# A gated cross-attention kernel on one core: turns and gate products put behind the projections, and an output bias added by GpSimd

## What is computed

```python
x = x + tanh(g_xattn[0]) * L0_xattn(layernorm(x), ctx)   # one head, 77 keys
x = x + tanh(g_ffn[0])   * L0_ffn(layernorm(x))          # 256 -> 1024 -> 256, quantised
x = x + tanh(g_xattn[1]) * L1_xattn(layernorm(x), ctx)   # 16 heads, out = concat @ Wo + bo
x = x + tanh(g_ffn[1])   * L1_ffn(layernorm(x))          # 8 experts, top 2, capacity 512
# L0_ffn: h = gelu_by_pieces(round(x @ w1 + b1)); out = round(h @ w2 + b2), rounded to 1/256
```

## Time and profile before

| | us |
|---|---|
| median of three executions | 490.95 (490.82 to 492.32) |
| profiled execution, its own time | 491.95 |
| its span in the trace | 490.2 |
| TensorE busy | 454.8 (93%) |
| VectorE busy | 370.4 (76%) |
| ScalarE busy | 258.6 (53%) |
| GpSimd busy | 145.6 (30%) |

### The profile page before, as it was taken

The page is one execution under the profiler, slowest core; times in us unless marked ns, Lnnn a source line. Parts: engine busy times, 40 slices in busy tenths (PEclk is TensorE's granted clock), DMA queues, the critical chain, the costliest instruction groups (busy, mean ns, idle before and its releaser), DMA issues.

```text
span 490.2 us, 8549 instructions
## 1 busy us (share of the span) xinstructions
PE 454.8 (93%) x3226; PEld 395.9 (81%) x3226; DVE 370.4 (76%) x753; ACT 258.6 (53%) x416; POOL 145.6 (30%) x122
## 2 busy tenths in 40 slices
PE   6999999999998999998997499999999999999991
PEld 4787789798887888787886259989999999999991
DVE  4689998898988978899898966686757475757441
ACT  2577899697965664556554132463434344442220
POOL 3354100010002211222113063215263645445153
PEclk9999999999999999999999799999999999999997
DMA  7412200000000101312123341134363747461031
GB/s 243 136 43 60 82 1 2 0 1 1 1 0 1 45 1 44 117 57 87 45 86 127 126 125 55 23 130 136 98 162 96 170 96 195 86 174 20 3 48 16
DMA packets 37135, 36.06 MB, mean 74 GB/s; under 512 B 6442, under 2 KB 35942, under 8 KB 36966
## 3 DMA queue, kind: packets, MB, share of 16 engines
q1 hardware_dynamic: 30633, 27.65, 17.3%
q0 software_dynamic: 6144, 7.66, 9.1%
q10 hardware_dynamic: 317, 0.21, 0.1%
HBM read 27.69 MB, written 8.39 MB: 74 GB/s over the span
## 4 chain that ended last, share of the span: by engine, by line
PE 75%; DVE 15%; issue 4%; DMA 2%; ACT 1%; POOL 1%; ACTq 0%; DVEq 0%; POOLq 0%
PE PS L1489 19%; PE PS L1490 18%; PE PS L1491 18%; PE PS L1898 5%; PE PS L1509 2%; DVE nmaxC L1181 2%; PE PS L1844 2%; PE PS L1909 2%; DVE xn L1020 1%; DVE tmp L1184 1%; DVE st L993 1%; DMA tmp<-in_L_xattn_Wk 1%; PE PS L1546 1%; PE PS L1760 1%; DVE tmp L1231 1%
## 5 line engine op out<-in xcount | busy, mean ns | idle before, releaser
L1489 PE MATMUL PS<-w_hi,hT_hi 128*128 128x256 f32 x384 | 110.3, 287 | 0.8 <-DVE hT_lo L1161 0.6
L1490 PE MATMUL PS<-w_lo,hT_hi 128*128 128x256 f32 x384 | 108.6, 283 | 0.0
L1491 PE MATMUL PS<-w_hi,hT_lo 128*128 128x256 f32 x384 | 108.6, 283 | 0.0
L964 ACT ACTIVATE tmp<-PS,biasT 128x512 f32<-128x512 f32 (+1 forms) x80 | 43.8, 600 | 111.1 <-PE PS L1491 111.1
L673 POOL DMA_INDIRECT out<-tmp,dst_idx x32 | 56.1, 1754 | 98.6 <-DVE tmp L1445 91.8
L1489 PE MATMUL PS<-xT_hi,w_hi 128*128 128x512 f32 (+1 forms) x224 | 81.6, 364 | 1.1 <-DVE xT_lo L1028 1.1
L1490 PE MATMUL PS<-xT_lo,w_hi 128*128 128x512 f32 (+1 forms) x224 | 80.8, 361 | 0.0
L1491 PE MATMUL PS<-xT_hi,w_lo 128*128 128x512 f32 (+1 forms) x224 | 80.4, 359 | 0.0
L1489 PEld LDWEIGHTS PS<-w_hi,hT_hi 128*128 128x128 f32 x384 | 73.4, 191 | 4.1 <-issue 2.2
L1490 PEld LDWEIGHTS PS<-w_lo,hT_hi 128*128 128x128 f32 x384 | 73.5, 191 | 0.8
L1491 PEld LDWEIGHTS PS<-w_hi,hT_lo 128*128 128x128 f32 x384 | 73.5, 191 | 0.0
(11 more groups left out here) (254 smaller groups left out, 819.9 us busy)
## 6 DMA issues: line engine op xcount, KB each, us to landing
w_raw<-in_L_ffn_w SPq DMA_DIRECT2D x72, 256.0 KB, 3.0
residual<-in_x SPq DMA_DIRECT2D x4, 512.0 KB, 5.3
out<-residual SPq DMA_DIRECT2D x3, 512.0 KB, 4.2
normed_rows<-xn SPq DMA_DIRECT2D x3, 512.0 KB, 3.6
kv<-in_L_ffn_b SPq DMA_DIRECT2D x1, 1024.0 KB, 6.5
tmp<-in_L_xattn_Wq SPq DMA_DIRECT2D x2, 256.0 KB, 5.4
out<-residual SPq DMA_DIRECT2D x2, 256.0 KB, 4.2
normed_rows<-xn SPq DMA_DIRECT2D x2, 256.0 KB, 3.1
```

The source lines that it names most:

```text
L964: act.activation(gD[:, G % 2, f, 0:P * n], H[:, G % 2, f, 0:P * n], ACT.Gelu, bias=biasT[:, col:col + 1]).then_inc(e_gelu, 1)
L1489: pe.matmul(o, lh, rh, start=start, stop=False, skip_group_check=skip)
L1490: pe.matmul(o, lh, rl, start=False, stop=False, skip_group_check=skip)
L1491: return pe.matmul(o, ll, rh, start=False, stop=stop, skip_group_check=skip)
```

## The change

- First feed-forward, TensorE: `output_bias`, `gate_weights` and `gate_constant` move from steps 3, 7 and 11 to steps 4, 8 and 12, and they and `transpose_x` now stand behind `project(g - 4)` instead of in front of it. The waits for ScalarE's copies of the gate pieces keep their steps (5, 9, 13) and move behind `project` too.
- ScalarE: the copies of the gate pieces move from steps 3, 6 and 10 to 4, 8 and 12; `x_hi` moves from `g % 4 == 0` to `g % 4 == 1`, `x_rest` from `g % 4 == 1` to `g % 4 == 2`, in front of `ffn_output`. VectorE's `centre_gate` moves from step 4 to 5.
- The bias products use 128 rows, of which all but two hold zeros; VectorE clears these rows once.
- Second attention: the output bias, already multiplied by the gate, is added to four tiles of the residual at a time by GpSimd, once their normalised rows exist. VectorE's `heads_out` goes; residual and logits read the bank directly, the bias of the logits is added to four tiles at a time in `rows_logits`, and TensorE waits for residual and logits before it overwrites the bank.

```diff
--- before.py
+++ after.py
@@ -187,7 +187,6 @@
         qT = view(4096, KD, 512)
         conc = view(6080, 2, D)
         concT = view(6592, 2, KD, P)
-        yC = view(7104, 2, D + NE)
         lgT = view(7632, 512)
         recC = view(8144, 2, HEADS)
         Kpar = kv[:, 0:8 * KEYS].rearrange("p (m b h k) -> p m b h k", m=KD, b=2, h=2)
@@ -239,7 +238,7 @@
 
         tg_unit = small[:, 19:20]
         woT = kv[:, 8 * KEYS:8 * KEYS + KD * D]
-        b2_hl, ones_b2 = w_lo[0:33, 7, 0, 0, :], w_lo[0:33, 7, 0, 1, 0:P]
+        b2_hl, ones_b2 = w_lo[:, 7, 0, 0, :], w_lo[:, 7, 0, 1, 0:P]
         b2_raw = b2_bc[0:33, :]
         ones_hl, bq_pad = w_hi[0:33, 7, 0, 0, 0:P], w_hi[0:33, 7, 0, 1, 0:2 * KP]
         bq_pad = bq_pad.rearrange("p (b k) -> p b k", b=2)
@@ -353,7 +352,7 @@
         c_ctr = sem("c_ctr")
         c_ctcopied = sem("c_ctcopied")
         c_wo = sem("c_wo")
-        c_wofree = sem("c_wofree")
+        bias_added = sem("bias_added")
         x3_ready = sem("x3_ready")
         out_init = sem("out_init")
         woT_copied = sem("woT_copied")
@@ -619,6 +618,14 @@
             power(NC + 3)
             power(2 * NC)
 
+            def add_output_bias(c):
+
+                pool.wait_ge(bo_ready, 1)
+                pool.wait_ge(xn_ready, round_of(2, c) + 1)
+                rows = xr[:, 4 * c:4 * c + 4, :]
+                pool.tensor_tensor(rows, rows, bcast(bo_bc[:, 0:D].unsqueeze(1), [P, 4, D]), ALU.add).then_inc(bias_added, 1)
+
+            add_output_bias(0)
             pool.wait_ge(hT_used, NB_PAIRS)
             flag = dict(allow_small_or_imprecise_dtypes=True)
             pool.iota(iota_e, pattern=[[1, NE]], base=0, channel_multiplier=0, **flag).then_inc(rt_consts, 1)
@@ -633,15 +640,18 @@
                 low_parts(PAIRS + i)
 
             power(round_of(2, 1))
+            add_output_bias(1)
             low_beside(0, 2)
             low_beside(1, 4)
             power(round_of(2, 2))
             low_beside(2, 6)
             power(round_of(3, 0))
+            add_output_bias(2)
             low_beside(3, 8)
             power(round_of(2, 3))
             low_beside(4, 10)
             power(round_of(3, 1))
+            add_output_bias(3)
             low_beside(5, 12)
             low_beside(6, 14)
             power(round_of(3, 2))
@@ -869,15 +879,16 @@
                                        bias=small[:, 16 + end:17 + end], scale=STEP).then_inc(gelu_ready, 1)
                     if g + 1 < NB_PAIRS:
                         to_grid(g + 1)
-                    if g == PAIRS - 1:
+                    if g == PAIRS:
                         act.wait_ge(bo_psum, 1)
-                        act.activation(bo_bc[:, :], T[:, 0, 0:D + NE], ACT.Copy).then_inc(bo_ready, 1)
+                        act.activation(bo_bc[:, 0:D], T[:, 0, 0:D], ACT.Copy, scale=tg[:, 1:2])
+                        act.activation(bo_bc[:, D:D + NE], T[:, 0, D:D + NE], ACT.Copy).then_inc(bo_ready, 1)
                         act.activation(woT, T[:, 1, :], ACT.Copy).then_inc(woT_copied, 1)
-                    if g == PAIRS + 2:
+                    if g == 2 * PAIRS:
                         act.wait_ge(wp_psum, 1)
                         act.activation(wo[:, :, D:D + NE], T[:, 0, 0:KD * NE].rearrange("p (k e) -> p k e", k=KD),
                                        ACT.Copy, scale=tg[:, 1:2]).then_inc(wp_ready, 1)
-                    if g == 2 * PAIRS + 2:
+                    if g == 3 * PAIRS:
                         act.wait_ge(wp_psum, 2)
                         act.activation(bo_bc[:, D:D + NE], T[:, 0, 0:NE], ACT.Copy).then_inc(wp_ready, 1)
                 if g == NB_PAIRS:
@@ -890,13 +901,13 @@
                         act.wait_ge(hT_used, k - 3)
                     act.activation(hT_hi[:, k % 4, :, :], hB[:, k % 2, :, :].bitcast(I32), ACT.Copy,
                                    scale=2.0 ** -8).then_inc(hhi_ready, 1)
+                if g < NB_PAIRS and g % PAIRS == 2:
+                    x_rest(r)
                 if g % PAIRS == 2 and PAIRS < g < NB_PAIRS:
                     ffn_output(g // PAIRS - 1)
                 if g < NB_PAIRS:
-                    if g % PAIRS == 0:
+                    if g % PAIRS == 1:
                         x_hi(r)
-                    if g % PAIRS == 1:
-                        x_rest(r)
                     if g % PAIRS == PAIRS - 1 and r < 2 * NC:
                         apply(r + 1)
 
@@ -1078,7 +1089,8 @@
             def output_units():
                 dve.wait_ge(late_loaded, 48)
                 dve.memset(ones_b2.bitcast(F32), 0.0)
-                link(dve.tensor_copy(b2_hl, b2_raw))
+                link(dve.memset(b2_hl.bitcast(F32), 0.0))
+                link(dve.tensor_copy(b2_hl[0:33, :], b2_raw))
                 for row in (0, 32):
                     dve.tensor_copy(ones_b2[row:row + 1, :], ones_bf[row:row + 1, :])
                 dve.tensor_tensor(b2_hl[32:33, :], b2_raw[32:33], b2_hl[32:33, :].bitcast(F32),
@@ -1211,7 +1223,7 @@
                     stats(2 * NC)
                 if g == 2 * PAIRS + 2:
                     shifts(2 * NC, 1)
-                if g == PAIRS:
+                if g == PAIRS + 1:
                     centre_gate()
 
 
@@ -1226,18 +1238,16 @@
                                   pv[:, :, 0:P].rearrange("p m (h d) -> p m h d", h=HH),
                                   bcast(rc.unsqueeze(3), [P, 2, HH, HD]), ALU.mult).then_inc(c_conc, 1)
 
-            def heads_out(s):
+            def heads_residual(s):
                 dve.wait_ge(c_wo, s + 1)
-                dve.tensor_tensor(yC[:, s % 2, :], AT1[:, 0:D + NE], bo_bc[:, :], ALU.add).then_inc(c_wofree, 1)
-                dve.wait_ge(c_wofree, s + 1)
-
-            def heads_residual(s):
-                dve.scalar_tensor_tensor(out=xr[:, s, :], in0=yC[:, s % 2, 0:D], scalar=tg[:, 1:2], in1=xr[:, s, :],
+                dve.wait_ge(bias_added, s // 4 + 1)
+                dve.scalar_tensor_tensor(out=xr[:, s, :], in0=AT1[:, 0:D], scalar=tg[:, 1:2], in1=xr[:, s, :],
                                          op0=ALU.mult, op1=ALU.add).then_inc(x3_ready, 1)
 
             def heads_logits(s):
+                dve.wait_ge(c_wo, s + 1)
                 dve.wait_ge(lg_copied, s // 4 + 1)
-                dve.tensor_tensor(logits[:, s, :], yC[:, s % 2, D:D + NE], logits[:, s, :], ALU.add).then_inc(lg_added, 1)
+                dve.tensor_tensor(logits[:, s, :], AT1[:, D:D + NE], logits[:, s, :], ALU.add).then_inc(lg_added, 1)
 
             def rows_logits(c):
                 r = round_of(2, c)
@@ -1246,6 +1256,9 @@
                 dve.wait_ge(lg_ready, c + 1)
                 dve.tensor_tensor(logits[:, here, :], LG, bcast(spread[:, :].unsqueeze(2), [P, 4, NE]),
                                   ALU.mult).then_inc(lg_copied, 1)
+                dve.wait_ge(lg_copied, c + 1)
+                link(dve.tensor_tensor(logits[:, here, :], logits[:, here, :],
+                                       bcast(bo_bc[:, D:D + NE].unsqueeze(1), [P, 4, NE]), ALU.add))
 
             def top_two(c):
 
@@ -1285,7 +1298,6 @@
                 if 1 <= t <= NT:
                     normalise(t - 1)
                 if 2 <= t <= NT:
-                    heads_out(t - 2)
                     heads_residual(t - 2)
                     heads_logits(t - 2)
                 if t == 0:
@@ -1316,7 +1328,6 @@
             dve.wait_ge(rstd_ready, r4 - NS + 1)
             dve.wait_ge(x3_ready, first + 1)
             dve.bn_stats(st[:, r4 % 2, 0, :], xr[:, first, :])
-            heads_out(NT - 1)
             heads_logits(NT - 1)
             top_two(4).then_inc(rt_rank, 1)
             heads_residual(NT - 1)
@@ -1719,7 +1730,7 @@
                 if p == 0 and g < NB_PAIRS:
                     pe.wait_ge(late_split, 2)
                     for half in range(2):
-                        pe.matmul(O[:, 2 * half:2 * half + 2, :], ones_b2, bcast(b2_hl.unsqueeze(1), [33, 2, D]),
+                        pe.matmul(O[:, 2 * half:2 * half + 2, :], ones_b2, bcast(b2_hl.unsqueeze(1), [P, 2, D]),
                                   start=True, stop=False, skip_group_check=True)
                 tile, count = step_of(g - NB_PAIRS)[2:4] if g >= NB_PAIRS else (0, 4)
                 alone = g >= NB_PAIRS + NG - PAIRS
@@ -1784,27 +1795,28 @@
                     hidden(g)
                     if g == 0:
                         attend_values(NC - 1)
-                    if g == PAIRS - 1:
+                if g == 2:
+                    pe.wait_ge(x1_ready, NT)
+                    keep_warm(6, 14)
+                if g >= LAG_B:
+                    project(g - LAG_B)
+                if g < NB_PAIRS:
+                    if g == PAIRS:
                         output_bias()
                     if g == PAIRS + 1:
                         pe.wait_ge(bo_ready, 1)
                         pe.wait_ge(woT_copied, 1)
-                    if g == 2 * PAIRS - 1:
+                    if g == 2 * PAIRS:
```

(16 more changed lines are left out.)

## The result

The changed kernel takes 499.16 us in the median (498.98 to 499.32, four executions), the kernel before 490.88 (490.72 to 492.32, four executions beside it): a ratio of 1.0162 [1.0142, 1.0181], slower by 8.3 us. The forecast was 495.3 with 498.8 as the upper end. Its profiled execution took 498.98 us, with a span of 497.2.

What follows compares the result with a forecast made beforehand. TensorE was taken to bound both stages, with VectorE close behind. First feed-forward +7.6 and second attention -3.3 gave +4.3: 496.25 us from the profiled execution, 495.3 against the median; range 492.0 to 498.8.

Steps and rivals of the forecast that it cites:

- fill: First feed-forward, step 0 to step 5: TensorE waits 1.3 and 4.1 on ScalarE's late copies, 5.4; less 0.4, +5.0.
- the turns' waits for normalised rows: First feed-forward: two TensorE waits for ScalarE's normalising, 1.00 us measured for one, both predicted to go, -2.0.
- +2.6: First feed-forward, step 5 to the queries: 5.4 of new waits, less 2.0 for old waits and 0.8 for bias products.
- rival (1): First feed-forward: TensorE's clock falls after its 4.1 us idle, adding 1.9, 497.2 us in all; chance 0.18.
- products run until shortly before: Argument against the clock falling: the idle is only 4.1 us, and TensorE works until shortly before it.
- Nothing on the path; uncovered, 2.4 each: Second attention: GpSimd's four bias additions, 2.38 each, delay nothing; if not hidden, 2.4 us each.
- -3.3: Second attention: less VectorE work shortens TensorE's waits and the chain to the routing, 3.3 us saved; ends -1.5 and -6.3.
- waits for remainder halves: Second attention: two TensorE waits on VectorE, 1.0 together; a remainder half was to gain 0.2.
- -0.39 a pair: First feed-forward: a 128-row bias pair costs TensorE 0.47 instead of 0.86; three of four count, -1.2.
- +7.6: Whole first feed-forward: 5.4 early and 5.4 later waits, less 2.0 and 1.2; bounds +5.2 and +8.8.

## Why the prediction missed: a clock held for unlikely, and additions priced at nothing

**What held.** The waits of TensorE for ScalarE's late copies, their places, their order and most of their sizes; those of the turns came out at about half.

| wait of | forecast | measured |
|---|---|---|
| subtraction, fill | 1.3 | 1.11 |
| hidden products of step 4 | 4.1 | 3.79 |
| subtraction of step 6, hidden products of 8 and 12 | 0.5 each | 0.35 each |
| turns of steps 9 and 13 | 0.8 each | 0.48, 0.37 |
| subtraction of step 10 | 1.5 | 1.36 |
| subtraction of step 14 | 0.8 | 1.68 (0.63 without GpSimd's additions) |

A copy took 1.01 us (1.0 was assumed), the turns' waits for normalised rows are gone, and putting the copies back undoes the whole loss. Without GpSimd's additions the brackets behind the fill sum to 3.9, against 5.4 forecast, and yet the steps there came out 0.5 higher (+3.1 against +2.6): a stop costs more than its bracket. Step 11's hidden products start 4.96 us after the projections begin (109.94 to 114.90), 3.34 in the kernel before (103.54 to 106.88), so 1.62 for a bracket of 1.36. Before a stop the last instruction is shown with its full modelled length (0.28), where otherwise the next one starts 0.12 behind it. So the forecast of these steps was near in part by luck: shorter brackets, and a cost of each stop that it left out.

**The step that failed in the fill** is that the sum held the clock at its upper level and left its fall to rival (1), given 0.18. The clock did fall, and the argument against it, that "products run until shortly before", is what the trace contradicts: the hidden products of step 3 ended at 59.5, and the stop of 3.79 us was followed by 0.50 over 64 to 67. Hidden products at that level cost 1.7 more (4.44 and 4.43 against 2.74), and keeping TensorE busy through the stop gave 1.8 in the spans, 1.5 of it in the fill, and 2.7 in the medians; the rival's price was 1.9. The fill's forecast with it is 5.0 + 1.7 = 6.7, measured 6.5. The rows that stood for the forecast were not near: a stop of 1.7 us that left the clock at 1.00 and one of 5.53 that lowered it. Of 4.1 they say nothing, so nearer to an even chance would have been fair.

**The step that failed for GpSimd** is the sentence "Nothing on the path; uncovered, 2.4 each". It looked at who waits for the additions by semaphores, and there it was right. It did not ask whether the two engines can run side by side. In the trace two VectorE instructions with two operands in SBUF could not: 1.22 became 3.43 and 0.19 became 1.27. The row that gave the price, 2.38, could not show it: beside that low part, from 181.12 to 183.50, VectorE's timeline has only instructions that read PSUM.

```profile
181.79 0.79 DVE L1181 TENSOR_REDUCE nmaxC<-PS 128x8 f32<-128x616 f32 x1
182.62 0.80 DVE L1184 TENSOR_TENSOR tmp<-PS,nmaxC 128x616 f32<-128x616 f32 x1
```

Cutting the additions' length gives 2.5 us back (its executions lie between 495.88 and 497.12), of which 1.1 in the last steps of the feed-forward (step 5 to the queries, +4.2 against +3.1) and about 1.1 at the turns ahead of the queries (L1533, 1.62 against 0.56). The Trainium skill ("SBUF — State Buffer", SBUF: two separate sides) states the mechanism: VectorE and GpSimd share a pair of ports, which the first to start holds for its whole instruction while the other is blocked. The trace agrees in both directions, VectorE blocked at 131.92 and 174.26, GpSimd at 131.08 and, with the addition moved, at 176.70. The prediction should have weighed this rule, and it left it out.

**The second attention.** -3.3 was forecast, and the stretch became 3.2 shorter; but this is -4.3 (140.31 to 136.00 in the kernel with the short additions) and about 1.1 of collision. Of the 4.3, 0.5 comes with the feed-forward's edits, which alone leave 139.78 of that stretch. The wait ahead of the routing fell as forecast, by 0.9 (1.39 to 0.45). Both waits for remainder halves went whole: the one of 0.68 that ends the first stretch, and the other of 0.36, where 0.2 was forecast. The first long wait, in the stretch that was to gain most, stayed (1.13 and 1.12): VectorE's gain came out one wait later than forecast.

**The bias products.** -0.39 a pair is right as the step's saving, and the Trainium skill's rule that was weighed against it ("TensorE: Matmul & The Clock Gate", Why this matters for your kernels) is not borne out: a pair adds 0.86 to its step with 33 rows, 0.46 with 128. Alone it gains nothing, as the run with the bias rows alone shows; with the moved turns the two together shorten the feed-forward up to the queries by the 3.2 expected. The Trainium skill ("TensorEngine Tiling (Array Packing)", Key Properties) says that changing between tiling modes drains TensorE, which would fit the part of the cost that lies in the products on either side of the pair; no run here shows that this is the cause.

**The sum.** Feed-forward +9.4 (forecast +7.6: the clock 1.7 or so), attention -3.6 without collisions (496.7 against the 500.3 that the ratio of 1.0191 gives; forecast -3.3), collisions +2.5 (forecast 0): +8.3. The three are differences between neighbouring kernels of one chain, so they must add up to the measured time; the test of the account is that each fits what its timeline shows. With rival (1) and the collisions the forecast would have been 495.3 + 1.9 + 2.5 = 499.7.

**Open.** With the first two additions moved, 0.5 us still separate the changed kernel from the one with short additions (497.2 and 496.7). The timelines put them at the turns ahead of the queries (1.09 against 0.56), behind VectorE's 0.5. No run splits these between the longer L1015 and the later power, and none shows why L1015, with one operand in SBUF, got longer where L1004 did not.

## What to carry to other kernels

When a producer on the bottleneck engine is moved later, do not move its consumer on another engine with it by habit: look at when the consumer is due. Here the turns could go behind the projections for nothing, since the copies came after them anyway; moving the copies one step later cost 10.55 us. Before handing VectorE's work to GpSimd, lay the two timelines over each other, and put the piece where VectorE reads PSUM or is idle. And price a new stop of TensorE of some microseconds as the stop and the slower products behind it.

## What the runs showed of the hardware

In the changed kernel the granted clock was still 1.00 during a stop of 3.8 us (60 to 63 us) and fell to 0.50 after work had resumed: the first products at 63.30 are shown with 0.50 and 0.43 us, those from 63.86 with 0.63. That moment is not fixed. In the run with the short additions it fell within a stop of the same length:

```profile
61.00:62.30 1.30, 0.00 (x0) 0.00 (x0) 1.27 (x2) 1.30 (x3) 0.00 (x0) 0.50 0.00 0
```

TensorE's timeline there begins with a product of 0.79, and the hidden products of step 4 take 5.20 us (62.32 to 67.52) instead of 4.43, so the low clock cost 1.7 us in one execution and 2.5 in the other:

```profile
62.32 0.79 PE L1500 MATMUL PS<-xT_hi,w_hi 128*128 128x512 f32 x1 [3.81 <-ACT xT_lo L721]
```

A VectorE instruction of 0.19 us over 32 columns can take 1.27 because a GpSimd instruction over 1024 started a moment earlier; what counts is the length of the other one, not its own.
